# A graph network kernel whose side work gets its own steps from tables, in shorter collecting parts

## The reference

```
scores[h]  = (x Wself[h]) (x Wother[h])^T            # 4 heads of 16
masked     = leaky(adj * scores, 0.2) / 4 + (adj == 0) * -1e9
attn       = softmax(masked, axis=-1) * (adj != 0)
x = layernorm(x + relu(attn @ (x Wv[h]) + bias))      # layer 0, heads side by side
x = layernorm(x + (adj + I) @ x / rowsum(adj + I))    # layer 1
x = layernorm(x + adj @ (x W2) + b2)                  # layer 2
x = layernorm(x + where(adj @ x > 0.5, 1, 0))         # layer 3
```

## Time and profile before

| what | value |
|---|---|
| median of 3 runs | 1537.56 us (1536.58 to 1537.99) |
| the profiled execution | 1541.21 us, of which the span from first to last instruction is 1539.1 us |
| PE busy | 1360.2 us, 88% of the span |
| DVE busy | 1240.7 us, 81% |
| ACT busy | 1223.2 us, 79% |
| POOL busy | 1053.1 us, 68% |
| mean granted TensorE clock | 0.946 of 2.4 GHz |

### The profile page before, as it was taken

The page is one execution under the profiler, slowest core; times in us unless marked ns, Lnnn a source line. Parts: engine busy times, 40 slices in busy tenths (PEclk is TensorE's granted clock), DMA queues, the critical chain, the costliest instruction groups (busy, mean ns, idle before and its releaser), DMA issues.

```text
span 1539.1 us, 20977 instructions
## 1 busy us (share of the span) xinstructions
PE 1360.2 (88%) x7296; PEld 683.8 (44%) x7296; DVE 1240.7 (81%) x1490; ACT 1223.2 (79%) x1404; POOL 1053.1 (68%) x562
## 2 busy tenths in 40 slices
PE   4798898999999999999989989998999989799766
PEld 2443344454444444544444544444444444345323
DVE  2779889787979889788887879887788788987864
ACT  1699799887988889788888879888798888888631
POOL 3177768678677767777676786787677776876411
PEclk9999899999999999999999999999899999999977
DMA  6734444243333433343442443344334334101000
GB/s 94 117 34 75 47 87 52 58 39 60 77 44 69 48 67 73 48 58 34 98 51 58 40 62 75 44 74 45 67 55 67 53 37 82 41 15 28 14 11 11
DMA packets 140879, 84.95 MB, mean 55 GB/s; under 512 B 100372, under 2 KB 130522, under 8 KB 140762
## 3 DMA queue, kind: packets, MB, share of 16 engines
q1 hardware_dynamic: 125542, 64.67, 19.7%
q0 software_dynamic: 14160, 18.51, 15.4%
q10 hardware_dynamic: 1072, 0.43, 0.1%
HBM read 103.33 MB, written 21.38 MB: 81 GB/s over the span
## 4 chain that ended last, share of the span: by engine, by line
PE 50%; ACT 12%; issue 12%; DVE 12%; POOL 10%; DMA 2%; SPq 1%; ACTq 0%; POOLq 0%; DVEq 0%
PE M L604 10%; PE Z L570 9%; PE M L659 9%; PE Z L577 8%; POOL LS L503 7%; ACT LS L751 6%; PE Z L588 5%; ACT LS L759 4%; DVE LS L913 3%; PE Z L673 3%; DVE RP L899 3%; PE Z L613 3%; DMA adj_cast<-in_adj_dram 1%; PE Z L727 1%; DVE X L983 1%
## 5 line engine op out<-in xcount | busy, mean ns | idle before, releaser
L503 POOL TENSOR_TENSOR LS<-LS,MB 125x1000 f32<-125x1000 f32 x372 | 867.1, 2348 | 339.2 <-DVE LS L913 272.3
L751 ACT ACTIVATE LS<-Z 126x1000 f32<-126x1000 f32 x576 | 576.8, 1002 | 154.1 <-PE Z L577 153.1
L899 DVE TENSOR_TENSOR RP<-LS,RP 125x1000 f32<-125x1000 f32 x480 | 575.6, 1199 | 84.8 <-ACT LS L751 63.3
L759 ACT ACTIVATE LS<-LS 125x1000 f32<-125x1000 f32 x576 | 596.9, 1037 | 51.9 <-POOL LS L503 32.9
L570 PE MATMUL Z<-AT,BI 126*126 126x500 fp8e4 x1152 | 378.0, 411 | 79.1 <-ACT LS L751 52.5
L577 PE MATMUL Z<-FS,FO 128*125 128x500 f16 x1152 | 356.2, 391 | 0.0
L604 PE MATMUL M<-LS,V 126*18 126x500 f32 x2304 | 317.3, 624 | 5.9 <-ACT LS L759 5.8
L570 PEld LDWEIGHTS Z<-AT,BI 126*126 126x126 bf16 x1152 | 127.7, 142 | 389.9 <-ACT LS L751 187.1
L913 DVE TENSOR_TENSOR LS<-LS,MB 125x1000 f32<-125x1000 f32 x204 | 293.0, 1441 | 5.0
L577 PEld LDWEIGHTS Z<-FS,FO 128*125 128x125 f16 x1152 | 165.8, 144 | 97.4 <-issue 17.6
L659 PE MATMUL M<-AT,XP 125*128 125x500 fp8e4 x756 | 192.9, 377 | 0.0
(11 more groups left out here) (133 smaller groups left out, 811.2 us busy)
## 6 DMA issues: line engine op xcount, KB each, us to landing
MB<-row_maxima SPq DMA_DIRECT2D x48, 500.0 KB, 4.0
adj_cast<-in_adj_dram POOLq DMA_DIRECT2D x96, 183.1 KB, 4.5
FO<-PARTS SPq DMA_DIRECT2D x120, 46.9 KB, 2.2
FS<-PARTS SPq DMA_DIRECT2D x120, 46.9 KB, 2.1
XF<-in_x_dram SPq DMA_DIRECT2D x8, 336.0 KB
XA<-in_x_dram SPq DMA_DIRECT2D x8, 336.0 KB
out_dram<-X SPq DMA_DIRECT2D x7, 375.0 KB
AT<-adj_cast SPq DMA_TRANSPOSE x144, 2.8
```

Source lines behind the costliest of these rows:

```text
L503: nc.gpsimd.tensor_tensor(rows, rows, MB[:P, u % 2, :, :], ALU.subtract).then_inc(sub_pool, 1)
L751: nc.scalar.activation(LS[:PD, q % RL, :, :], banks("Z", q)[:PD], ACT.Prelu, alpha=SLOPE).then_inc(bent, 1)
L759: nc.scalar.activation(rows, rows, ACT.Exp, scale=0.25).then_inc(exps, 1)
L899: nc.vector.tensor_tensor(run, rows, run, ALU.max).then_inc(maxed, 1)
```

## The change

The offsets become tables: each event of a graph has its own step. Collecting goes in CUTS = 4 parts of 3 tiles, 12 parts a layer in place of 9. The subtractions move from 18 to 19 steps behind the fill, the exponents from 20 to 21 and the weighing from 22 to 23. The turning of the matrix on SP is cut into three pieces of two transfers, and the pieces have steps of their own. Within a step, the order of the events changes too: PE turns the sums before collecting and turns the maxima last; ACT makes the high halves before the bend; DVE scales first; POOL takes the low halves first and loads last.

```
-CUTS = 3
+CUTS = 4
-LAG = 18
-SUB_AT = LAG + 0
-EXP_AT = LAG + 2
-WEIGH_AT = LAG + 4
+POOL_AT, SUB_AT, EXP_AT, WEIGH_AT = 19, 19, 21, 23
-RT_AT = STEPS + MAX_AT + 1
-TAKE_AT = STEPS - 1 + WEIGH_AT + 0
-G_AT = TAKE_AT + 2
-KEEP_AT = G_AT + 0
+TURNED = (15, 15, 14, 15, 15, 15)
+MAXIMA = (15, 15, 14, 14, 15, 14)
+SPREAD = (16, 16, 16, 15, 15, 15)
+TAKE = (35, 35, 35, 34, 34, 34)
+SUMS = (36, 36, 36, 36, 35, 35)
+KEEP = (35, 35, 35, 36, 35, 35)
-MEANS = (25, 42, 61, 79)
-CENTRE, SQUARE, SUM, POWER, SCALE, HIGH, LOW, Y0, W0 = 1, 2, 2, 3, 4, 5, 5, 9, 12
+MEANS = (24, 44, 63, 85)
+CENTRE = (25, 45, 67, 86)
+SQUARE = (26, 47, 66, 87)
+SUM = (26, 46, 66, 88)
+POWER = (28, 49, 66, 89)
+SCALE = (28, 49, 67, 90)
+HIGH = (29, 51, 69)
+LOW = (30, 50, 70)
+COLLECT = ((33, 34, 35, 36, 37, 38, 39, 40, 41, 42, 43, 44),
+           (53, 54, 55, 56, 57, 58, 59, 60, 61, 62, 63, 64),
+           (72, 73, 74, 75, 76, 77, 78, 80, 81, 82, 83, 84))
...
+BACK = ((37, 42, 46),
+        (58, 61, 65),
+        (76, 82, 85))
+ADD = ((37, 42, 45),
+       (57, 62, 65),
+       (76, 82, 85))
+FEATURES = (14, 18, 19, 20, 22, 23, 27, 30, 32)
...
+LOWER = (17, 23, 29)
...
-TRANSPOSES = {3: 1, 15: 2, 47: 3}
+SLICES = ((2, 2, 4), (15, 16, 18), (44, 44, 44))
+CUT_Q = 3
...
-                for q in range(NQ):
+                for q in range(NQ * k // CUT_Q, NQ * (k + 1) // CUT_Q):
...
+                if layer_at(q, LOW):
+                    low(*layer_at(q, LOW))
+                if layer_at(q, POWER):
+                    power(*layer_at(q, POWER))
+                e = q - POOL_AT
+                if 0 <= e < QN and not by_vector(e):
+                    subtract(e)
                 if load_at(q) and load_at(q)[0] >= NS:
                     load(*load_at(q))
...
+                if q < QN:
+                    fill_z(q)
+                if unit_at(q, SUMS) is not None:
+                    turn_sums(unit_at(q, SUMS))
+                if rows_at(q, COLLECT):
+                    lb, l, n = rows_at(q, COLLECT)
+                    collect(lb, l, *divmod(n, CUTS))
+                if feature_at(q, FEATURES, KINDS):
+                    make_features(*feature_at(q, FEATURES, KINDS))
+                if rows_at(q, BACK):
+                    turn_back(*rows_at(q, BACK))
                 e = q - WEIGH_AT
                 if 0 <= e < QN and e % 2:
                     weigh(e // 2)
+                u = turned_at(q, TURNED, LAST_RT)
+                if u is not None:
+                    turn_run(u)
```

More of the change, by code:

```diff
@@ L219, in adj_resnorm, with unit_at, turned_at @@
         block = ctx.enter_context(nc.Block())
[L221 to L228, removed]
         def graph_at(q):
             return divmod(q, SPG)
+        def unit_at(q, steps):
+            for u in range(max(q // STEPS - 4, 0), min(q // STEPS + 1, NU)):
+                if STEPS * u + steps[u % UPG] == q:
+                    return u
+            return None
+        def turned_at(q, steps, last):
+            if q >= last:
+                return NU - 1 if q == last else None
+            u = unit_at(q, steps)
+            return u if u != NU - 1 else None
         def load_at(q):
@@ L244, in slice_at, with ones_at, parts_at, layer_at @@
             b, r = graph_at(q)
-            if r not in TRANSPOSES:
-                return None
[L247 to L253, removed]
+            for s, steps in enumerate(SLICES):
+                for k, at in enumerate(steps):
+                    if at == r and NS * b + s + 1 < NS * B:
+                        yield NS * b + s + 1, k
+        def ones_at(q):
+            b, r = graph_at(q)
+            if r not in ONES_AT or NS * b + ONES_AT.index(r) + 1 >= NS * B:
+                return None
+            return NS * b + ONES_AT.index(r) + 1
+        def parts_at(q):
+            b, r = graph_at(q)
+            for n, steps in enumerate(HEADS_AT):
+                bb = b + (n >= 2)
+                for side in range(2):
+                    if steps[side] == r and bb < B:
+                        yield bb, (n + 2) % H, side
+        def layer_at(q, steps):
+            for l, at in enumerate(steps):
+                b, off = divmod(q - at, SPG)
                 if off == 0 and 1 <= b < B:
@@ L256, in layer_at, with rows_at, feature_at @@
             return None
[L258 to L263, removed]
-            return None
[L266 to L273, removed]
+        def rows_at(q, steps):
+            for l in range(NS):
+                for n, at in enumerate(steps[l]):
+                    b, off = divmod(q - at, SPG)
+                    if off == 0 and 1 <= b < B:
+                        return b - 1, l, n
+            return None
+        def feature_at(q, steps, kinds):
             b, r = graph_at(q)
-            if r in FEATURES and b + 1 < B:
-                kind, c = FEATURES[r]
+            if r in steps and b + 1 < B:
+                kind, c = kinds[steps.index(r)]
                 return kind, b + 1, c
@@ L396, in _ @@
             sp.wait_ge(ones_in, 1)
-            turn_slice(0)
+            for k in range(CUT_Q):
+                turn_slice(0, k)
             add_ones(0)
@@ L1102, in _ @@
                     centre(*at)
-                if layer_at(q, SCALE):
-                    scale(*layer_at(q, SCALE))
-                if w_at(q):
-                    add_up(*w_at(q))
-                at = layer_at(q, 0)
-                if at and at[1] in CENTRED:
-                    mean(*at)
-                if layer_at(q, SUM):
-                    add_squares(*layer_at(q, SUM))
+                if unit_at(q, KEEP) is not None:
+                    keep(unit_at(q, KEEP))
                 e = q - SUB_AT
@@ L1116, in _ @@
                     neighbours(b - 1)
+                if rows_at(q, ADD):
+                    add_up(*rows_at(q, ADD))
+                at = layer_at(q, MEANS)
+                if at and at[1] in CENTRED:
+                    mean(*at)
                 if q == LAST_ROWS:
```

157 lines of the change are left out of this document (68 added, 89 removed).

## The result

| | before | after |
|---|---|---|
| median on the same chip | 1541.83 us (1536.58 to 1547.76, 11 runs) | 1533.36 us (1530.38 to 1538.38, 11 runs) |
| ratio | | 0.9945, 95% interval 0.9925 to 0.9965 |
| profiled execution, its span | 1541.21, 1539.1 us | 1531.98, 1529.9 us |

Faster by 0.55%, some 8.5 us. The forecast had 1514 us and 1.5%: the sign and the wide range (1482 to 1550) held, the forecast's own range (1498 to 1526) did not, and the size was less than half.

The account below looks back on a forecast made before the run. DVE was taken to bound steps outside collecting, PE the collecting. 3.3 + 1.0 - 0.5 = 3.8 us a graph: 27 less over seven graphs, 3 more at the ends, 1514 us; own range 1498 to 1526, 8-in-10 range 1482 to 1550.

Parts of the forecast that it names:

- So DVE sets these stretches, PE the collecting: Steps outside collecting: DVE's events sum to 103.4 us against 102.41 measured, so DVE bounds them; PE bounds the three collecting stretches.
- Collecting, 3.3 us a graph: 36 of 72 steps now collect: collecting stretches 93.3 us, the others 83.4, sum 176.7, a gain of 3.3 us a graph.
- a rival that would take the gain away: "No change": collecting stretches start at half PE clock, losing 3.8 us a graph, all the gain: 1541 us; chance 0.10.
- One of its signs of being wrong: Listed observations that would show the forecast wrong, among them a granted clock under 0.94 in collecting.
- The graph that was read: One graph's 72 steps, cut into six stretches, 179.95 us long, from which the forecast took its per-graph times.
- POOL's third normalisation, 1.0 gained: POOL's work in steps 64 to 67 took 12.7 us for 10.0; now 14.7 against 15.0; 1.0 us a graph taken.
- the rule that the prediction gave 0.12: DVE's two-SBUF-input subtractions and POOL's subtractions exclude each other: gain 1.9 us a graph, 1528 us; chance 0.12.
- Waits that come in on DVE, 0.5 lost: Four new DVE waits for PE's turned maxima, sums or features: 0 to 8.2 us a graph, 0.5 taken.
- The rival "slower": DVE does not cover the four new waits, 8.2 us a graph at one ACT step each: 1568 us; chance 0.18.
- SP, nothing: Four transposing transfers ahead of the sixth unit's maxima: 8.9 us against 10.0 for four steps, so nothing lost.
- Ends, 3 lost: First graph's subtractions start 2.1 us later, one more DVE subtraction at the end: 3 us, between 0 and 6.

## Why the prediction was wrong

**The step that failed** is the sentence "So DVE sets these stretches, PE the collecting". It rested on a sum of DVE's events, 103.4 us against 102.41 measured, with 1.25 us for each maximum. The match was chance. The rows that it stood on had the answer: in the three stretches that don't collect PE was busy 56.99 + 15.42 + 19.05 = 91.5 us, DVE 91.2 and ACT 92.6, all three nine tenths of 102.4. No bound can be read from three engines that are equally busy, and taking 4.1 us of DVE's work a graph out of the longest stretch gave nothing. That DVE was behind ACT at seven of eight maxima says only that DVE ran late, not that anybody waited for it. In the forecast's sum 27 us were to come from seven graphs and 3 to be lost at the ends: 14.1 came from six, nothing from the seventh, and 4.9 were lost.

**Collecting, 3.3 us a graph: measured 1.0** (7.2 us for seven graphs). The stretches came out near the forecast (96.94 less 0.9 for step 7 is 96.0, for 93.3; the others 80.9, for 83.4), and yet the reason was another. PE has the same tiles to collect in 12 parts or 9, so a step moved into collecting isn't won. In the table the whole steady gain stands in the column of the clock: 6.3 us a graph less at 1.2 GHz, worth 3.1 (the estimate of the work is up by 0.8, which I can't explain), and the idle time as before. The same column holds what the longer parts cost: 8.7 to 10.8. The forecast named idle time and DVE's load; it put the clock at nothing and spoke of it only as a rival that would take the gain away. One of its signs of being wrong did come, a clock under 0.94 in collecting (0.92 in the third stretch).

**The graph that was read.** Rows 1 cover one graph of 179.95 us. The six have 178.7 in the mean, and the changed graphs 176.3, where the forecast came to 176.15. So 1.2 us of each 3.8 were in the choice of one slow graph, and that the changed graphs came to the forecast's length is luck; the last graph, for which 3.8 were counted too, gained nothing (171.7 to 172.1 us to its last fill).

**POOL's third normalisation, 1.0 gained: right as far as it went.** The stop of step 68 went, and PE's idle time in steps 60 to 71 fell from 3.95 to 2.26 us a graph. As the idle time of a whole graph is the same, it came back elsewhere (in steps 0 to 32, 5.6 us before and 8.1 now). The lower halves now shut DVE's subtraction out, and keeping them apart gave some 0.5 to 1 us a graph. This is the rule that the prediction gave 0.12. Its mechanism holds at this place, but its total doesn't explain the result, since the exclusion costs the kernel before more (24 us for 15); that its 1528 us lies nearer to the result than 1514 is chance.

**Waits that come in on DVE, 0.5 lost.** DVE's waits for turned maxima grew from 63.7 to 73.6 us over the whole run, about 1.2 a graph. What that costs was not measured by itself. The rival "slower" rested on the same sentence as the forecast, DVE as the bound, and fell with it. Not counted at all were new waits on ACT, for the slice copied at step 74, for features and for DVE's subtractions: 10.4, 7.5 and 6.3 us in five graphs. Taking the first away alone, and the first two with the lower halves later, gave nothing that can be measured.

**SP, nothing:** right. POOL's waits for `MB` grew from 40.3 to 54.7 us, 4.6 of that in the longest, at the start; with whole transposes behind the maxima the time is the same.

**Ends, 3 lost: 4.9** (4.0, 0.7 and 0.2). It isn't the lag, as the kernel with the lag alone has a first graph of 148.5 us. One trace is a rough measure: where the first graph is that of the kernel before it took 149.6 to 153.3 us, in four traces, and where it is that of the changed kernel 155.8 to 158.6, in five. In the first graph PE's idle time grew from 24.5 to 29.2 us and its time at 1.2 GHz from 25.9 to 40.2. Which of the moved events does it was not tried.

**What stays open:** which property of a stop makes the clock fall. The same idle time lies in shorter stops now: the five longest are 3.13, 1.41, 1.39, 1.33 and 1.33 us in the mean before, 1.47, 1.22, 1.04, 1.02 and 0.94 after. That fits fewer falls, and so does filling them, but some falls come behind stops of 0.6 us and some stops of 1 us have none behind them. The changed kernel's own gain was not taken away by giving it the old stops back. One profiled execution stands for each kernel in the table; over all runs the mean granted clock agrees in direction, 0.944 before (106 runs), 0.953 after (11), 0.971 with the stops filled (6).

## What to carry to other kernels

Where several engines are nine tenths busy in the same stretch, don't name a bound from a sum that happens to match: cut one engine's work in a few steps and see whether the time moves. Add up the engine whose work can't change first (here PE: work, idle time, time at the lower clock), over several repeats and not one, and ask of a change which of the three it touches. A stop of PE can cost a second time by the clock behind it, so before moving work to close a stop, fill it with matmuls that change nothing and measure: here that gave 21 us in one kernel and nothing in another.

## What the runs showed of the hardware

- 256 more matmuls made a kernel 21 us faster: the granted clock over its six graphs rose from 0.96 to 0.99, and a part of them took the place of idle time (13.4 us a graph before, 9.6 with them).
- A subtraction of DVE with two SBUF inputs made next to no progress while POOL issued its load and made the lower halves: 3.17 us for 1.19, ended 1.06 us after POOL. Beside a subtraction, a load and lower halves of POOL it took 4.47. Reading one input from PSUM it took 1.18 to 1.20 everywhere.
- In 106 runs of the kernel before, time and mean granted clock go together (correlation -0.67): 0.01 of clock is some 6 us.
